# Moving x and normalised x of the read phase as sixteen all-partition pieces a block, with the tables loaded first and half a projection placed ahead of a variance sum

## What is computed

```python
m = mean(x); v = var(x); xn = (x - m) / sqrt(v + eps)            # over 2048
y = einsum('blhc,hoc->bloh', xn.reshape(b, l, H, C), W)           # three reads
yn = (y - mean(y)) * rsqrt(var(y) + EPS) * gamma + beta           # over 512
q, k, v = (einsum('bli,oi->blo', yn[s], qkv_w[s]) for s in range(3))
q, k = rope(q, pos), rope(k, pos)
```

## Time and profile before

| | |
|---|---|
| median of 3 runs (lowest to highest) | 2234.54 us (2231.17 to 2235.7) |
| the profiled execution | 2232.62 us, span 2230.7 us |
| PE busy | 1980.0 us, 89% of the span |
| DVE, ACT, POOL busy | 1422.7, 979.8, 424.4 us |
| read phase (about) | 28 to 370 us of the span |

### The profile page before, as it was taken

How to read it: one execution, slowest core, us unless ns; L and a number is a source line. 1 busy time by engine, 2 the same in 40 slices (tenths; PEclk the granted TensorE clock), 3 DMA queues, 4 the chain that set the end, 5 groups by cost and what they waited for, 6 DMA issues and landing times.

```text
span 2230.7 us, 25094 instructions
## 1 busy us (share of the span) xinstructions
PE 1980.0 (89%) x9562; PEld 1374.4 (62%) x9562; DVE 1422.7 (64%) x1563; ACT 979.8 (44%) x1376; POOL 424.4 (19%) x325
## 2 busy tenths in 40 slices
PE   2689987899999997369989999999999999989997
PEld 0144555566655553237767777777777677766786
DVE  3656866777777773966856738748639658478100
ACT  3555753578777875226136143044331152431100
POOL 1000003575556670000000001110001000011111
PEclk8799997799999998679999999999999999999999
DMA  8847355676776753236755757876658777568675
GB/s 202 175 104 166 89 121 180 223 271 242 243 242 239 257 181 125 97 137 219 262 204 219 285 179 214 258 249 235 234 188 219 230 248 266 218 191 253 156 178 138
DMA packets 180924, 453.85 MB, mean 203 GB/s; under 512 B 64321, under 2 KB 64577, under 8 KB 165441
## 3 DMA queue, kind: packets, MB, share of 16 engines
q1 hardware_dynamic: 146592, 313.52, 42.1%
q0 software_dynamic: 32480, 128.46, 20.6%
q10 hardware_dynamic: 1728, 10.22, 1.3%
HBM read 304.80 MB, written 147.32 MB: 203 GB/s over the span
## 4 chain that ended last, share of the span: by engine, by line
PE 42%; DVE 7%; DMA 5%; ACT 4%; issue 2%; SPq 0%; POOL 0%; DVEq 0%; ACTq 0%; POOLq 0%
PE ps L1773 16%; PE ps L1583 7%; PE ps L1585 7%; PE ps L1584 7%; DMA sign_h<-sign_h_scratch 3%; DMA up<-up_s_scratch 2%; PE ps L1642 1%; PE ps L1651 1%; ACT L1802 1%; PE ps L1603 1%; DVE Y L2096 1%; PE ps L1692 1%; PE ps L1680 1%; ACT E_attn L1826 0%; ACT E_mlp L1826 0%
## 5 line engine op out<-in xcount | busy, mean ns | idle before, releaser
L1773 PE MATMUL ps<-XH,sign_h 128*128 128x512 f32 x768 | 306.5, 399 | 13.4 <-DMA sign_h<-sign_h_scratch 8.9
L1773 PE MATMUL ps<-XL,sign_h 128*128 128x512 f32 x768 | 300.3, 391 | 0.0
L1148 DVE TENSOR_REDUCE maxes<-ps 128x1 f32<-128x512 f32 (+3 forms) x384 | 207.7, 554 | 96.5 <-PE ps L961 73.6
L1583 PE MATMUL ps<-ZH,up 128*128 128x512 f32 x512 | 204.3, 399 | 16.1 <-DVE ZL L2121 8.9
L1585 PE MATMUL ps<-ZH,up 128*128 128x512 f32 x512 | 200.4, 391 | 0.0
L1584 PE MATMUL ps<-ZL,up 128*128 128x512 f32 x512 | 200.3, 391 | 0.0
L1075 ACT ACTIVATE probs<-ps 128x512 f32<-128x512 f32 (+3 forms) x384 | 167.5, 486 | 50.2 <-PE ps L988 29.9
L1773 PEld LDWEIGHTS ps<-XH,sign_h 128*128 128x128 f32 x768 | 144.8, 189 | 60.1 <-issue 13.6
L958 PE MATMUL ps<-turned_k,turned_q 96*128 96x512 f32 (+3 forms) x384 | 157.3, 422 | 12.1 <-DVE maxes L1148 10.9
L1004 PE MATMUL ps<-probs,v_ones 128*64 128x512 f32 (+3 forms) x768 | 167.2, 513 | 0.3 <-ACT probs L1075 0.3
L1773 PEld LDWEIGHTS ps<-XL,sign_h 128*128 128x128 f32 x768 | 144.8, 189 | 31.3 <-issue 1.9
(11 more groups left out here) (334 smaller groups left out, 4180.4 us busy)
## 6 DMA issues: line engine op xcount, KB each, us to landing
sign_h<-sign_h_scratch SPq DMA_DIRECT2D x256, 256.0 KB, 3.8
up<-up_s_scratch SPq DMA_DIRECT2D x58, 1024.0 KB, 6.3
proj<-proj_s_scratch SPq DMA_DIRECT2D x58, 640.0 KB, 4.0
X<-in_x POOLq DMA_DIRECT2D x16, 1024.0 KB, 15.5
xn_scratch<-X SPq DMA_DIRECT2D x16, 1024.0 KB, 14.2
sign_raw<-in_sign SPq DMA_DIRECT2D x32, 512.0 KB, 8.0
sign_h_scratch<-sign_high SPq DMA_DIRECT2D x32, 512.0 KB, 4.1
sign_l_scratch<-sign_low SPq DMA_DIRECT2D x32, 512.0 KB, 5.3
```

Of the source, the lines that this page charges most:

```text
L1148: eng.tensor_reduce(MAXES[:, e, q, k0 // T:k0 // T + 1], ps[:, MX[m % 2], 0:w], AX.X, ALU.max).then_inc(mx_read.sem, mx_read.unit)
L1583: eng.matmul(out_ap, lh, rh, start=start, stop=False, skip_group_check=True)
L1773: mm = eng.matmul(ps[:, sign_bank(m)], s[q][:, f], x[:, n], start=n + w == 0, stop=n == NF - 1 and w == len(operands) - 1, skip_group_chec ...
```

## The change

Five edits. (1) The load and the store of a block of X are sixteen transfers, one for each feature tile, over all 128 partitions, where they were four, one for each c, over 32 partitions. The bytes are the same: 4 x 1 MiB become 16 x 256 KiB. On the DRAM side a piece is 4 x 32 rows of 2 KB. (2) In the setup, POOL waits for the six tables before it loads x, and ACT issues three of the six. (3) The variance of block 0 is summed in bank YV instead of XS, so that `x_var(0, 0)` does not wait for the last centring. (4) `project(0, 0)` is cut in two, and its first half stands ahead of `x_var(1, 0)`. (5) The counts of the semaphores follow.

```diff
-def rows_of_x(t, x_c, c, n):
-
-    q = P // C
-    return (t["X"][c * q:(c + 1) * q, n % 2], x_c[c][:, :, n * T:(n + 1) * T])
+def rows_of_x(t, x_f, f, n):
+
+    return (t["X"][:, n % 2, f], x_f[f][:, :, n * T:(n + 1) * T])
...
             @block.gpsimd
             def _(eng):
-                for c in range(C):
+                eng.wait_ge(loaded.sem, loaded.at(k=len(loads)))
+                for c in range(NF):
                     eng.dma_start(*rows_of_x(t, io["x_c"], c, 0)).then_inc(t["x_in"][0].sem, t["x_in"][0].unit)
 
             @block.sync
             def _(eng):
-                for dst, src in loads:
+                for dst, src in loads[:3]:
...
+                for dst, src in loads[3:]:
+                    eng.dma_start(dst, src).then_inc(loaded.sem, loaded.unit)
                 eng.wait_ge(dve.sem, dve.at(k=15))
...
-        xn_out = [ev(f"xn_out{a}", per=C, unit=16) for a in range(2)]
+        xn_out = [ev(f"xn_out{a}", per=NF, unit=16) for a in range(2)]
...
                     eng.wait_ge(x_act.sem, x_act.at(n, X_SQUARED + g))
-                    if g == 0:
+                    if g == 0 and n:
                         eng.wait_ge(xn.sem, xn.at(n, HC))
-                    quarters(XS, lambda j: t["ones_p"][:], SQX[g % 2], g == 0, g == HC - 1).then_inc(xv.sem, xv.unit)
+                    quarters(XS if n else YV, lambda j: t["ones_p"][:], SQX[g % 2], g == 0, g == HC - 1).then_inc(xv.sem, xv.unit)
...
                 y_var_close(0, 1)
+                project(0, 0, 0, 2)
                 x_var(1, 0)
                 x_var(1, 1)
-                project(0, 0)
+                project(0, 0, 2, TT)
...
-        io[name] = [rows[c * HC:(c + 1) * HC].rearrange("a (j h) t -> h (a j) t", j=C) for c in range(C)]
+        io[name] = [rows.rearrange("(c a) (j h) t -> a j c h t", c=C, j=C)[f // C, f % C] for f in range(NF)]
```

More of the change, by code:

```diff
@@ L253, in _ @@
                     half = n % 2
-                    eng.wait_ge(xn_out[half].sem, xn_out[half].at(n // 2 - 1, C))
+                    eng.wait_ge(xn_out[half].sem, xn_out[half].at(n // 2 - 1, NF))
                     eng.wait_ge(rd.sem, rd.at(n - 2, 3 * HC))
-                    for c in range(C):
+                    for c in range(NF):
                         eng.dma_start(*rows_of_x(t, io["x_c"], c, n)).then_inc(x_in[half].sem, x_in[half].unit)
@@ L268, in store @@
                                   OUT[:, tt].rearrange("p (h a d) -> p h a d", h=NH // 2, a=1)).then_inc(stored[tt].sem, stored[tt].unit)
-                eng.wait_ge(x_in[0].sem, x_in[0].at(0, C))
+                eng.wait_ge(x_in[0].sem, x_in[0].at(0, NF))
                 eng.dma_start(t["read1"][:], io["read1"]).then_inc(w_in.sem, w_in.unit)
@@ L285, in _ @@
                 for half in range(2):
-                    eng.wait_ge(xn_out[half].sem, xn_out[half].at(NB // 2 - 1, C))
+                    eng.wait_ge(xn_out[half].sem, xn_out[half].at(NB // 2 - 1, NF))
                 for tt in range(TT):
@@ L301, in x_mean @@
                 def x_mean(n):
-                    eng.wait_ge(x_in[n % 2].sem, x_in[n % 2].at(n // 2, C))
+                    eng.wait_ge(x_in[n % 2].sem, x_in[n % 2].at(n // 2, NF))
                     past(eng, x_act, n - 1, X_RSTD)
@@ L463, in x_copy @@
                         eng.wait_ge(xv.sem, xv.at(n, HC))
-                    eng.activation(R[:, 0], ps[:, XS], ACT.Copy).then_inc(x_act.sem, x_act.unit)
+                    eng.activation(R[:, 0], ps[:, XS if n or k == 1 else YV], ACT.Copy).then_inc(x_act.sem, x_act.unit)
                 def x_square(n, g):
@@ L512, in z_high @@
                     if z_place(n, s):
-                        eng.wait_ge(xn_out[0].sem, xn_out[0].at(NB // 2 - 1, C))
+                        eng.wait_ge(xn_out[0].sem, xn_out[0].at(NB // 2 - 1, NF))
                         eng.wait_ge(rd.sem, rd.at(NB - 2, 3 * HC))
@@ L2253, in build @@
                 t["X"] = sbf("X", [P, 2, NF, T])
-                t["x_in"] = [Count(first, nc, f"x_in{half}", per=C, unit=16) for half in range(2)]
+                t["x_in"] = [Count(first, nc, f"x_in{half}", per=NF, unit=16) for half in range(2)]
                 setup_phase(nc, io, t)
```

## The result

The changed kernel takes 2280.18 us (median of 4 runs, 2278.18 to 2288.8) where the kernel before takes 2233.36 in the same comparison (4 runs): a ratio of 1.0213, 95% interval 1.0187 to 1.024. It is slower, as forecast, but by 47 us and not by 134. The profiled execution took 2278.18 us, with a span of 2276.4 (before: 2230.7).

The account below looks back on a forecast made before the run. PE was taken to bound the whole span (1980.0 of 2230.7 us). With stores at 77 us a block, the first stage ends 132.6 + 2.9 = 135.5 us later, savings included; on the profiled 2232.62 that is 2368, range 2211 to 2395.

Parts of the forecast that it names:

- The stores' mechanism: Stores of normalised x on SP: outermost size 4 puts each on the same four engines; forecast at price near 77, chance 0.50.
- the nearest row is the store of normalised x itself: 77: Stores of normalised x: four engines at the old store's 310 engine-us a block take 77 us a block.
- the other bound: Stores of normalised x on four engines at the weights load's price: 160 / 4 = 40 us a block.
- the 10 us that I gave to sixteen engines: Stores of normalised x on all sixteen engines: 10 to 19.3 us a block; rival case 2208 to 2228, chance 0.25.
- four engines at the full price: Rival on the stores: 40 us a block, sum +10.4, 2243 us (2235 with fast loads); chance 0.25.
- The load of x: Block 0's start: transfer still takes 24.7 us, x lands at 28.9 and PE starts 1.0 us later.
- Four pieces in flight fill sixteen: POOL's loads of x: pieces use four engines each, four in flight fill sixteen, so no more than +1.0 us at the start.
- The rival gain by the issue price (-6.5): Block 0's load of x: at 0.86 us an issue x lands at 21.3 and PE starts 6.5 us sooner.
- Tables first: Setup: tables land by 4.2 us, DVE's work on them ends at 15.1, POOL starts x at 4.2 instead of 1.36.
- Variance bank: Block 0's variance: squares no longer wait for all four centrings, -3.3 us.
- Half projection: Ahead of block 1's variance: 24 matmuls fill PE's idle time, -5.1 us, bounds 0 and -6.5; 7 at half clock.
- no gain for x of block 3: PE's wait for x in block 2: no gain if the load takes 24.7 us, -6.2 us if it is fast.

Follow-up runs that it names:

- rows outermost: Changed kernel, still 16 pieces over 128 partitions, partition index row by quarter so DRAM has 32 outermost, reading weights laid out to match: 2216.65 us, ratio 0.9923.
- stores alone in pieces: Changed kernel with its loads of x back in four transfers of 32 partitions, only the stores in 16 pieces: 2251.57 us, ratio 1.0089.
- the pieces of 32 partitions: Changed kernel with 16 pieces of 256 KB a block, each over 32 partitions, 32 x 4 x 512 in DRAM: 2224.65 us, ratio 0.9968.
- the rest alone: Changed kernel with the four transfers of before; tables first, variance bank and half projection kept: 2222.57 us, ratio 0.9956.

## Why the prediction was right in sign and wrong in size

**The stores' mechanism: right.** With an outermost 4 SP's queue has a share of 24.4% of the sixteen engines, with 2 it is 13.1% and with 32 it is 102.5%: in size the shares of four, two and all sixteen. That is the rule of the Trainium skill, "DMA: Bandwidth & Descriptors", section "Why a DMA increments its semaphore by 16 and not by 1", and the runs agree with it at 2, 4 and 32 for SP's stores, and at 4 and 32 for SP's load (26.2% and 81.6%).

**The stores' price: the step that failed.** It is "so the nearest row is the store of normalised x itself: 77". A block's store takes 41 us at its steady rate, near the 160 / 4 = 40 of the other bound. I had read the earlier trace rows as "a transfer over 32 partitions is slow", 74 against 38 engine-us a MB, and carried the 74 to four engines. But stores over 128 partitions also take 75 on sixteen engines, stores over 32 take 69 to 74, and on four or two engines it is 41. So the 74 belongs to sixteen engines storing at once, at 200 to 240 GB/s in all, and not to the partitions; four engines at 102 GB/s are far below that. The same fault underlay the 10 us that I gave to sixteen engines as the low end: it is about 20. What sets the 200 to 240 GB/s of a store stays open; it is a mean, and the 40 slices of 58:68 with rows outermost run from 156 to 393 GB/s once the store is under way. The 38 was a load of weights, in the other direction, and that it comes so near to the 41 is in part luck. The 77 also leaned on the Trainium skill, "SBUF — State Buffer", the section on the DMA port swizzle, by which partitions p and p + 32 share a port. That engines on such partitions would double each other's price was my inference, and the 41 engine-us a MB on four engines refutes it at that size. A smaller price no run here excludes, since with two engines the shares lie 32 partitions apart as well.

**The sum.** Replacing 77 by 40 was the rival "four engines at the full price", 2243. The run with the stores alone in pieces is that rival, at 2251.57. It is some 9 us above, because the stores took 43 us of data after some 2 us and not 40: q's store was waited for three times and for 24.0 us, where the rival's sum had two waits of 4.3 and 7.7.

**The load of x: under-priced.** This is the second term that was mis-sized. I took 24.7 us for it in pieces of 4 x 32 rows, and let it count for 1.0 us at the start. It takes 33 to 37. That is the rest of the way from 2252 to 2280: 10.5 us at the start, and longer waits in blocks 2 and 3. The row that I had named as dear, 129 engine-us a MB for POOL's stores, pointed that way: at the measured 108, the 4.19 MB are 28 us of all sixteen engines, before any start or end. "Four pieces in flight fill sixteen" was right (94.2%), but it says nothing of what a piece costs. Rows outermost (57 engine-us a MB, the same partitions) and the pieces of 32 partitions (75) show that it is the outermost 4 (108), with the same number and size of issues: 1106 packets for 3.61 MB and 1109 for 3.64 against 4146 for 4.20. The small packets, of 4 or 8 bytes, come with that form on POOL's queue. Their own time is not the loss: by the single packets of the trace they take 43 of the 452 engine-us in 6:36, while a data packet of 4096 bytes takes 401 ns on average there, against 302 in 8:25 of the pieces of 32 and 230 in 8:22 with rows outermost. Why the data packets are slow, and whether the small ones between them slow them, stays open. The rival gain by the issue price (-6.5) did not come: even with rows outermost the load takes 20.8 us from the first issue to PE's start.

**Tables first: right in what it does.** DVE starts at 3.95 (forecast 4 to 5) and ends at 15.7 (15.1), and with the old transfers PE starts exactly 1.0 us later.

**Variance bank: right.** 3.2 and 3.4 us against 3.3; ACT's copy comes 12.0 us after the first centring starts (13). **Half projection: right in kind, a little large.** 4.1 and 4.6 us against 5.1. PE's gap ahead of it is 3.89 us (4), but 14 of its 24 matmuls run at the lower clock, 0.43 us apart and granted 0.50 in 108:113, where I had 7; then they come 0.23 us apart, granted 1.00 in 114:116. Less the 1.0 of the tables, variance and half projection make 6.8 of the 8.0 us by which the rest alone reaches attention earlier; its median gains 10.6 (2233.15 to 2222.57), with an interval from 6 to 13. The forecast of no gain for x of block 3 was right here, since it is late by more than before. "No gap above 2.2 us" missed one of 2.91 us before 128.59, a wait for block 1's scaling; nothing was worked out from it. But a saving was not passed on in full, as I had taken it to be: with the transfers slow, the wait for x in block 2 took it back.

**The number.** 2280 is inside my range of 2211 to 2395, but that says little: it lies between the ranges of the two four-engine cases (2232 to 2260 and 2310 to 2400), and a store at 41 us with a load at 33 to 37 was in neither.

**The signs.** POOL's wait for the store was 60.59 us (forecast 75), PE waited for x of blocks 2 and 3, and DVE for q's stores, all as named; the GB/s was near 102 and not near 54, which is the sign that tells the two prices apart.

## What to carry to other kernels

Before cutting a transfer differently, look at the outermost size on both of its sides, the DRAM side too: a dimension of 4 put outermost cost this kernel 63 us, and putting the 32 outermost, with the operand that reads it laid out to match, turned a loss of 2.1% into a gain of 0.8%. A price per MB that was read while sixteen engines worked together must not be divided by fewer engines: it may be the price of their crowd. And measure the pieces one at a time: here a gain of 8 us was hidden under two losses of 24 and 29, and beside both of them it was all but gone (0.8 us at attention), since a wait for a transfer takes back what the engines saved ahead of it.

## What the hardware showed that I had not expected

- A store from SBUF over sixteen engines runs at 200 to 240 GB/s whether it covers 32 or 128 partitions (74, 69 and 75 engine-us a MB), and at 41 engine-us a MB on two or four engines (51 and 102 GB/s).
- A load of the same 4.19 MB by POOL does depend on the form: 108 engine-us a MB for 4 x 32 rows over 128 partitions, 75 for 32 x 4 rows over 32 partitions, 57 for 32 x 4 rows over 128.
- With an outermost 4, POOL's queue keeps all sixteen engines busy (94.2%) where SP's queue uses a quarter (26.2% for the same load). POOL's load then has some 3100 packets under 512 B, against some 220 with 32 outermost, and its data packets take 401 ns in place of 230 or 302.
- A store issued on SP's queue while POOL's load keeps the engines busy barely starts: 0.9% beside 102.4% in 69:78.
- SP issues no faster than its stores drain once a few are in flight: 2.44 us (median) for an issue of 256 KB on four engines, 2.45 for one of 128 KB on two, 0.61 for one of 256 KB on sixteen.
